# Turning the per-head sums and the row maxima with full-precision identity products in 32-column tiles

## The reference

```python
q = heads(x @ Wq)
out_short = softmax(q @ k_s.T / sqrt(16) + decay_bias) @ v_s     # decay_bias = -|i - j| * (1 - decay)
out_long  = softmax(q @ k_l.T / sqrt(16)) @ v_l
out = sigmoid(mix) * out_short + (1 - sigmoid(mix)) * out_long
x1 = layernorm(x + out @ Wo)
```

## Time and profile before

| | |
|---|---|
| median of 3 runs | 2228.13 us (2227.36 to 2230.89) |
| profiled execution, its own time | 2229.06 us |
| span of its profile | 2227.3 us |
| TensorE products busy | 2067.9 us, 93% |
| TensorE weight loads busy | 1121.7 us, 50% |
| VectorE busy | 1652.0 us, 74% |
| ScalarE busy | 1470.1 us, 66% |
| GpSimd busy | 171.8 us, 8% |
| mean granted TensorE clock | 0.966 |

### The profile page before, as it was taken

One profiled execution on the slowest core, in us unless ns is written; L12 is line 12 of the kernel. 1 busy time (PEld: TensorE's weight loads), 2 busy tenths in 40 slices (PEclk: granted clock), 3 DMA queues, 4 the chain that ended last, 5 costly groups with the idle time before them and its releaser, 6 DMA issues.

```text
span 2227.3 us, 42640 instructions
## 1 busy us (share of the span) xinstructions
PE 2067.9 (93%) x16472; PEld 1121.7 (50%) x16472; DVE 1652.0 (74%) x2107; ACT 1470.1 (66%) x1758; POOL 171.8 (8%) x202
## 2 busy tenths in 40 slices
PE   4999999999999999999999999999999879999940
PEld 2444444444444444444444444444444358888840
DVE  4788888888888888888888888888888633333367
ACT  1677777777777777777687777777777732333336
POOL 0000000000000000000000000000000000000038
PEclk7899999999999999999999999999999979999975
DMA  4222222222222222222222222222222130000017
GB/s 100 50 56 55 64 57 63 56 64 56 64 56 64 57 63 56 64 65 56 65 54 64 56 63 57 64 65 55 56 55 55 36 116 29 19 28 28 19 44 220
DMA packets 128201, 134.27 MB, mean 60 GB/s; under 512 B 39810, under 2 KB 86658, under 8 KB 128018
## 3 DMA queue, kind: packets, MB, share of 16 engines
q1 hardware_dynamic: 97650, 97.59, 18.6%
q10 hardware_dynamic: 30368, 34.18, 5.1%
HBM read 37.77 MB, written 16.78 MB: 24 GB/s over the span
## 4 chain that ended last, share of the span: by engine, by line
PE 87%; ACT 4%; DVE 3%; issue 2%; POOL 2%; ACTq 1%; DMA 0%; POOLq 0%; SPq 0%; DVEq 0%
PE pv_ps L675 21%; PE pair_ps L612 17%; PE work L580 15%; PE pair_ps L637 12%; PE gate_ps L1151 12%; PE work L741 3%; PE pair_ps L588 3%; PE work L1144 2%; ACT probs L376 2%; DVE maxes L547 1%; ACTq L229 1%; POOL veps L905 1%; POOL rstd L907 1%; PE work L1135 1%; PE work L745 1%
## 5 line engine op out<-in xcount | busy, mean ns | idle before, releaser
L547 DVE TENSOR_REDUCE maxes<-pair_ps 128x2 f32<-128x1024 f32 x1024 | 1228.4, 1222 | 238.4 <-PE pair_ps L588 154.5
L376 ACT ACTIVATE probs<-pair_ps,small 128x1024 f32<-128x1024 f32 x512 | 563.2, 1113 | 227.2 <-PE pair_ps L588 225.7
L376 ACT ACTIVATE probs<-pair_ps 128x1024 f32<-128x1024 f32 x512 | 516.8, 1024 | 159.5 <-PE pair_ps L612 154.3
L675 PE MATMUL pv_ps<-probs,vals 128*32 128x512 f32 x4096 | 546.5, 605 | 0.2 <-ACT probs L376 0.2
L612 PE MATMUL pair_ps<-q_op,k_op 56*128 56x512 f32 (+1 forms) x2048 | 479.4, 477 | 13.8 <-ACT probs L376 10.6
L637 PE MATMUL pair_ps<-k_op,q_op 55*128 55x512 f32 x2048 | 435.8, 433 | 5.4 <-ACT probs L376 4.6
L612 PEld LDWEIGHTS pair_ps<-q_op,k_op 56*128 56x128 f32 (+1 forms) x2048 | 191.7, 184 | 444.3 <-DVE maxes L547 204.7
L637 PEld LDWEIGHTS pair_ps<-k_op,q_op 55*128 55x128 f32 x2048 | 196.5, 187 | 150.0 <-issue 106.5
L588 PE MATMUL pair_ps<-eye_b,tri_b 64*128 64x64 bf16 x4096 | 163.3, 194 | 0.0
L588 PEld LDWEIGHTS pair_ps<-eye_b,tri_b 64*128 64x128 bf16 x4096 | 94.2, 96 | 115.4 <-issue 99.1
L320 POOL TENSOR_TENSOR o_sum<-o_att 128x512 f32<-128x512 f32 x32 | 41.1, 1285 | 1280.0 <-DVE o_att L522 1280.0
(11 more groups left out here) (139 smaller groups left out, 2487.1 us busy)
## 6 DMA issues: line engine op xcount, KB each, us to landing
k_op<-kq_h SPq DMA_DIRECT2D x1024, 32.0 KB, 2.0
k_op<-kq_l SPq DMA_DIRECT2D x512, 32.0 KB, 2.0
q_op<-kq_h SPq DMA_DIRECT2D x496, 32.0 KB, 2.0
x_step<-in_xT ACTq DMA_DIRECT2D x16, 512.0 KB, 4.2
x_res<-in_x ACTq DMA_DIRECT2D x16, 512.0 KB, 4.7
x_dram<-res ACTq DMA_DIRECT2D x16, 512.0 KB, 3.4
x_back<-x_dram SPq DMA_DIRECT2D x16, 512.0 KB, 4.8
out<-summed SPq DMA_DIRECT2D x16, 512.0 KB, 3.1
```

Of the source, the lines that this page charges most:

```text
L376: act.activation(probs[:, s % 2, 2 * hp:2 * hp + 2, :], pairs_ps[pair_of(b, s, "b", hp)][:, :, :], ACT.Exp, scale=LAM if s // 4 % 2 else 1 ...
L547: dve.reduce_max(maxes[:, u % 2, :, hp, s % 4], pairs_ps[pair_of(b, s, "a", hp)][:, :, :], mybir.AxisListType.X).then_inc(a_reduced, 1)
L675: last = pe.matmul(pv_ps[32 * h:32 * h + 32, :], vals[:, c, g // 2, att, at:at + 32], probs[:, s % 2, h, :], start=(c == 0), stop=(c == TC ...
```

## The change

The turns by `pe.transpose` become ordinary fp32 matmuls with the same identity as moving operand. Each chunk of the sums is cut into four pieces of 32 columns of the stationary operand, which give partitions 0-31, 32-63, 64-95 and 96-127 of the output, the shape and the positions of the tiles that `weigh` uses. The maxima's 16 columns are one product. The waits, the order and the signal are as before; the turn of `o_sum` (L728) and that in the recurrence stay `transpose`.

```diff
-HALF = P // 2
+HALF, QUARTER = P // 2, P // 4
...
+            def turn_over(out, src):
+                for at in range(0, P, QUARTER):
+                    last = pe.matmul(out[at:at + QUARTER, :], src[:, at:at + QUARTER], id_sb[:, :], start=True, stop=True)
+                return last
...
                         for t in range(TC):
-                            last = pe.transpose(work[:, P * t:P * t + P], pv_sb[:, sums[1] % 2, P * t:P * t + P], id_sb[:, :])
+                            last = turn_over(work[:, P * t:P * t + P], pv_sb[:, sums[1] % 2, P * t:P * t + P])
                     if maxima:
                         wait(pe, a_reduced, maxima[0], 8 * UNITS, 8 * maxima[1] + 8)
-                        last = pe.transpose(turned_maxima, maxes[:, maxima[1] % 2, :, :, :].rearrange("p a h t -> p (a h t)"), id_sb[:, :])
+                        last = pe.matmul(turned_maxima, maxes[:, maxima[1] % 2, :, :, :].rearrange("p a h t -> p (a h t)"), id_sb[:, :],
+                                         start=True, stop=True)
                     last.then_inc(full["turn"], 1)
```

## The result

The changed kernel takes 2273.68 us (median of four, 2270.53 to 2274.31) against 2228.86 us for the kernel before in the same rounds: a ratio of 1.0198, 95% interval 1.018 to 1.0215. It is 44.8 us slower; the forecast was 2272 us. The profiled span grew from 2227.3 to 2272.2 us, by 44.9.

What follows compares the result with a forecast made beforehand. TensorE was taken to pace the attention loop. 128 turns at 0.38 us more gave 48.6 us, less 5 us net given back, so +44 us and 2272 us; range 2256 to 2288 us, chance 0.74.

Steps and rivals of the forecast that it cites:

- The pace: Attention loop: TensorE paces it, so a longer turn lengthens the run by nearly all of the difference.
- The wave: In the turn: four 32-column tiles side by side, 128 columns in two passes, take 0.108 us.
- The sum: Each turn: 1.105 us comes, 0.725 us goes, so 0.38 us more, 48.6 us over 128 turns.
- The gap and the load behind the maxima: Between maxima and weighted sums: the 0.15 us change-over goes and the 0.025 us load slips behind the maxima.
- the upper end: Between maxima and weighted sums: if the change-over stayed, 0.15 us a turn, 19 us more.
- The signal: Turn's end: signalled later, moving VectorE's steps on the bank by 0.1 us against TensorE.
- What is given back: Loop waits of TensorE: 7 us back and 2 us lost, 5 us net; bounds 0 and about 25 us back.
- (a): Turn: weight loads do not hide behind 0.107 us streams; +81 us less 5, 2304 us; chance 0.12, including a change-over that stays.
- (b): Turn: tiles don't keep side by side over 32 instructions; +159 us, 2380 to 2390 us; chance 0.05.
- (c): Loop: ScalarE or VectorE sets the pace, TensorE's idle time absorbs the longer turn; 2228 to 2245 us; chance 0.05.
- (d): Turn: identity products need one pass in each instruction, 0.054 us a wave; -20 us, 2208 us; chance 0.04.

Runs made afterwards that it cites:

- the doubled sums: The change with the 16 pieces of the sums made twice into the same place: 2385.23 us, ratio 1.0702, +111.5 us on the change.
- the whole-array product: The change with the sums by full-precision products of the whole array, 128 x 128, not in 32-column tiles: 2298.41 us, ratio 1.0308.
- another order of the same pieces: The change with all four chunks of the first tile issued first, then all four of the second, and so on: 2424.57 us, ratio 1.0878.

## Why the prediction was right

**The pace.** TensorE paces the loop, and the difference in its stretch reaches the end: shown by the table over ten kernels, and by the doubled sums most plainly.

**The wave.** The sum had 0.108 us for 128 columns in two passes, a quarter of L675's. The rows give (0.90 - 0.03) / 8 = 0.109. Eight waves and two for the maxima were the whole of the cost, and the whole-array product shows that they are passes and not instructions or tiles. The sum had 0.38 us a turn; the median over all turns is 0.375. It multiplied by 128, where 126 turns hold both halves.

**The gap and the load behind the maxima** went, as said: on the maxima's own tile L682 begins 0.11 us after their last product, without either. The sum split their old 0.20 us into 0.053 of stream and 0.15 of gap, which was wrong: the rows above give 0.11 and 0.09. It cost nothing, as the sum took away the whole 0.20 us; only the upper end, with its 19 us for a gap that stays, should have been 12 us. The Trainium skill's rule in "TensorEngine Tiling (Array Packing)", "Key Properties", that a change of tiling mode drains the array, agrees with these traces as to a gap of 0.09 to 0.12 us between unlike kinds; but the runs show the same gap between the weighted sums and a one-pass product whose output has 16 partitions, and none between that and an old turn.

**What I had not foreseen** is that three of the four weighted sums start beside the maxima (1036.11, x3). So the first of them comes 0.90 us after the turn's start and only the fourth 1.11 us after it, where I had set 1.05 to 1.15 for the first. It bought nothing: the next scores are of another kind and wait for the last tile, which is the one that the maxima held.

**The signal.** VectorE's first step now starts 0.20 us after the last of the weighted sums' first wave; in the earlier trace rows it was 0.11 us after their start. So it is late by 0.09 us, for 0.1 said.

```profile
1036.52 0.28 DVE L512 TENSOR_SCALAR shift_rows<-work 16x128 fp32r<-16x128 f32 x1 [0.45 <-PE work L752]
```

**What is given back** was the weak term. I had 7 us back, mostly from waits for `probs`, and 2 us lost on `o_att`. Waits of the products in the loop, then two of the whole run:

```profile
PE pair_ps L619 <- ACT probs L376: 10.6, 24, 1.4
PE work L587 <- ACT pv_sb L431: 10.3, 16, 0.8
PE pair_ps L644 <- ACT probs L376: 4.6, 8, 0.8
```

```profile
DVE shift_rows L512 <- PE work L752: 49.2, 97, 4.2
...
PEld work L580 <- DVE o_att L522: 5.2, 14, 0.4
```

The waits for `probs`, 10.6 and 4.6 us, are the same to a tenth as in the earlier trace rows, and those for `pv_sb` are 10.3 us, where they were 10.1. They did not shrink, which is not what I had said; why is not shown. Those on `o_att` fell from 8.9 us to 5.2, though the signal comes later; VectorE itself waits more for the turn, 97 times. What did come back were waits for `maxes`. Before, a turn in most batches reads:

```profile
985.17 0.66 PE L741 MATMUL work<-ident_sb,pv_sb 128*128 128x128 f32 x4
...
987.08 0.49 PE L612 MATMUL pair_ps<-q_op,k_op 56*128 56x512 f32 x2 [0.15 <-DVE maxes L547]
```

Here the stretch is 1.91 us, set by VectorE, in 15 of the 126 turns; the median is 1.69. In the change no turn is above 2.07 and the line on `maxes` of the earlier trace rows is gone. 15 times 0.22 is 3.3 us, where I had 5 net from other waits. That the forecast came within 2 us of the median is partly luck: 48.6 less 5 was to stand against 47.3 less 3.3, and the two errors nearly cancel.

**The rivals.** (a), loads that show: out, by the pitch of 0.109 and, more strictly, by the whole-array products, whose loads are four times as wide and hide too, at a pitch of 0.112. So the rule of the Trainium skill, "TensorE: Matmul & The Clock Gate", "The mechanism", that loads overlap only products of another row group, does not hold for these runs. (b), tiles that don't run side by side: out for the change, and yet it is the rival with most behind it, as another order of the same pieces costs 151 us. (c), absorption: out, but for those 15 turns, where VectorE took in 0.22 us of each. (d), one pass in each instruction for an identity: out, as the wave was 0.109 us and not 0.054.

## What to carry to other kernels

Where TensorE paces a loop, price an edit as the stretch between two fixed neighbours in its timeline, gaps between unlike kinds of product included: at about 0.1 us each, they made half of this edit dearer than all of it, and a cheaper product in the wrong place dearer than the one it replaced. A turn by a full-precision product costs four passes of its columns (0.22 us for 128), the old turn half of that, and narrow tiles make it no cheaper; they pay by joining a neighbour of the same kind. Hand products out to the tiles in turn: four for one tile in a row cost nothing here, six and eight did.

## What the runs showed of the hardware

- Each column tile took three products waiting behind its running one, and later instructions for other tiles had to wait behind a full tile. It gives 3.18, 2.09 and 2.53 us for three orders; 3.25, 2.07 and 2.60 were measured. The rule fits three orders and was laid down before the third was run; that it is a queue for each tile is the reading that fits, not something that a row shows directly.
- As to gaps, the kernels show two kinds at 128 rows: full-precision products in 32-column tiles on one side; on the other old turns and a one-pass product of 16 columns. That whole-array full-precision products are not of the first kind follows from one gap of 0.10 us ahead of the maxima; whether they are of the second was not tested.
- Weight loads of 128 columns hide behind full-precision products of 128 columns but for 0.003 us (pitch 0.112 us against 0.109 in narrow tiles).
- An old turn of 128 columns holds the array for 0.11 us, about two passes of 0.053 us, also when the load behind it has 16 columns and not 128.
